# Two attention layers with exact row maxima: one rotation of three PSUM banks for row scores and turned maxima, and the narrow bias products of layer 1 in one run

## The reference, cut to what matters

```python
Q, K, V = split(query @ Wq.T + bq), split(key @ Wk.T + bk), split(value @ Wv.T + bv)   # 16 heads of 16
scores = einsum("bhqd,bhkd->bhqk", Q, K) / 4       # 512 x 1024 for each head and batch
scores = where(mask, -inf, scores)                 # layer 0: a boolean mask
scores = scores + attn_mask                        # layer 1: an additive mask; both: softmax over k
out = einsum("bhqk,bhkd->bhqd", softmax(scores), V) @ Wo.T + bo
x = x + out
```

## Time and profile before

| | |
|---|---|
| median of three runs | 1301.94 us (1301.23 to 1302.68) |
| the profiled execution: own time, span | 1301.66 us, 1299.9 us |
| mean granted TensorE clock | 0.943 |
| TensorE, VectorE, ScalarE, GpSimd busy | 89%, 44%, 35%, 16% of the span |
| steps of layer 0, from the first head product | 104.4 to 343.2 us |
| opening of layer 1 in attend | 672.8 to 707.4 us |
| steps of layer 1 | 707.4 to 967.8 us |

### The profile page before, as it was taken

The page is one execution under the profiler, slowest core; times in us unless marked ns, Lnnn a source line. Parts: engine busy times, 40 slices in busy tenths (PEclk is TensorE's granted clock), DMA queues, the critical chain, the costliest instruction groups (busy, mean ns, idle before and its releaser), DMA issues. The chain is left out here.

```text
span 1299.9 us, 19266 instructions
## 1 busy us (share of the span) xinstructions
PE 1158.5 (89%) x7144; PEld 714.0 (55%) x7144; DVE 568.1 (44%) x1587; ACT 452.6 (35%) x584; POOL 205.3 (16%) x334
## 2 busy tenths in 40 slices
PE   5777999999959999999667999999996499999993
PEld 3432333333447888888533223322225499999993
DVE  5465777774263111112356676666505311111112
ACT  4344666666412111121033455555662011111110
POOL 4362222223100000000013000000200111111110
PEclk9998999999959999999878899999997699999997
DMA  7527222200273334445069022220003699998943
GB/s 222 135 106 174 37 38 37 38 1 1 98 260 49 130 129 138 179 176 137 24 225 173 1 37 38 38 38 1 1 2 131 219 369 313 316 319 317 313 150 106
DMA packets 95878, 169.45 MB, mean 130 GB/s; under 512 B 8529, under 2 KB 65569, under 8 KB 94770
## 3 DMA queue, kind: packets, MB, share of 16 engines
q1 hardware_dynamic: 89570, 157.59, 40.5%
q0 software_dynamic: 2208, 6.03, 1.6%
q10 hardware_dynamic: 4016, 4.72, 1.1%
HBM read 148.34 MB, written 19.79 MB: 129 GB/s over the span
## 5 line engine op out<-in xcount | busy, mean ns | idle before, releaser
L1042 ACT ACTIVATE prob<-st_ps 128x1024 f32<-128x1024 f32 x256 | 261.0, 1025 | 192.9 <-PE st_ps L938 107.7
L131 DVE CUSTOM_DVE_ANT_0 junk<-s_ps,bias_rows,mx 128x512 f32<-128x512 f32 x236 | 172.2, 750 | 72.7 <-PE s_ps L116 72.5
L116 PE MATMUL s_ps<-k_stack,q_stack 97*128 97x512 bf16 x468 | 181.3, 392 | 12.6 <-DMA q_stack<-q_scr 6.6
L930 PE MATMUL st_ps<-q_stack,k_stack 100*128 100x512 bf16 x512 | 185.5, 386 | 6.9 <-ACTq L1021 6.9
L131 DVE CUSTOM_DVE_ANT_0 junk<-s_ps,bias_rows 128x512 f32<-128x512 f32 x232 | 156.2, 690 | 75.9 <-PE s_ps L116 72.7
L1429 PE MATMUL h_ps<-expert_in,w 128*128 (+1 forms) x704 | 155.0, 382 | 2.3 <-PEq L64 2.3
L1429 PEld LDWEIGHTS h_ps<-expert_in,w 128*128 128x128 f32 (+1 forms) x704 | 132.7, 189 | 23.0 <-issue 2.5
L950 PE MATMUL o_ps<-prob,v_unit 128*32 128x512 f32 x1024 | 140.6, 603 | 0.5 <-ACT prob L1042 0.5
L116 PEld LDWEIGHTS s_ps<-k_stack,q_stack 97*128 97x128 bf16 x468 | 45.0, 98 | 166.4 <-DVE mx L131 136.6
L1832 ACT ACTIVATE silu<-gu_ps 128x512 f32<-128x512 f32 x46 | 27.5, 597 | 226.7 <-PE gu_ps L1788 226.7
L935 PE MATMUL st_ps<-bias_hi,ident_bf 128*128 128x512 bf16 x256 | 97.9, 382 | 0.0
(11 more groups left out here) (270 smaller groups left out, 1121.7 us busy)
## 6 DMA issues: line engine op xcount, KB each, us to landing
wg<-in_gateT SPq DMA_DIRECT2D x23, 1024.0 KB
wu<-in_upT SPq DMA_DIRECT2D x23, 1024.0 KB
wd<-in_downT SPq DMA_DIRECT2D x23, 1024.0 KB
w<-in_w SPq DMA_DIRECT2D x16, 1368.0 KB
k_stack<-k_scr SPq DMA_DIRECT2D x96, 128.0 KB, 4.9
w<-in_w SPq DMA_DIRECT2D x8, 1280.0 KB
k_scr<-k_parts SPq DMA_DIRECT2D x24, 256.0 KB, 2.5
q_stack<-q_scr SPq DMA_DIRECT2D x96, 64.0 KB, 4.9
```

The lines of the kernel that those rows point to most:

```text
L116: pe.matmul(self.ps[:, j % 2], stack(self.pr.Q[b], MROW, i % 2, h, slice(qt * P, (qt + 1) * P)), stack(self.pr.K[b], MROW, i % 2, h, slice ...
L131: self.pr.nc.vector.tensor_tensor_reduce(out=self.junk[:, j % 2], in0=self.ps[:, j % 2], in1=self.m.bias_rows[:, qt, half * 512:(half + 1) ...
L930: pe.matmul(st_ps[:, h], stack(K[b], ROWS, i % 2, h, slice(kt * P, (kt + 1) * P)), stack(Q[b], ROWS, i % 2, h, slice(0, SQ)), start=True, ...
L1042: nc.scalar.activation(prob[:, kt % 2, 2 * hp:2 * hp + 2], st_ps[:, 2 * hp:2 * hp + 2], ACT.Exp).then_inc(exp_done, 1)
```

## The change

`RowPass` (of `attend`; the opening of layer 0 keeps it, with `FirstMax` for its turns) and `MaxSteps` become one class, `RowRing`. It writes out the order of all row products and turns of a layer as TensorE will issue them, and gives them three banks in rotation. Each waits until the one three places before is read: a job's maximum, or a turn's write. The bank `m_ps` is gone; a turn no longer waits for the write of the turn before as such. GpSimd's five steps are the same (`split_max`). Two semaphore increments of a job (`passed`) and a memset fall away. In layer 1, the order of a step becomes h0 r0 h1 h2 r1 h3 r2 b0 b1 b2 b3, turn, weigh, r3. Layer 0 keeps its order.

```diff
+TURN_AT = (3, 6)
-            pe.wait_ge(self.done, u * 32 + j + 1)
-            pe.matmul(self.ps[:, j % 2], stack(self.pr.Q[b], MROW, i % 2, h, slice(qt * P, (qt + 1) * P)),
+class RowRing:
+    BANKS = 3
...
+        order = []
+        if first == 0:
+            order += [("job", 0, j) for j in range(32)] + [("turn", 0, 0), ("turn", 0, 1)]
+        for u in range(NU):
+            for kt in range(KT):
+                order += [("job", *x) for x in plan[u, kt][:3]]
+                if u + 1 < NU and kt in TURN_AT:
+                    order.append(("turn", u + 1, TURN_AT.index(kt)))
+                order += [("job", *x) for x in plan[u, kt][3:]]
+        self.order, self.place = order, {x: n for n, x in enumerate(order)}
+    def bank(self, *x):
+        return self.place[x] % self.BANKS
+    def free(self, pe, *x):
+        n = self.place[x] - self.BANKS
+        if n >= 0:
+            kind, u, i = self.order[n]
+            if kind == "job":
+                pe.wait_ge(self.done, u * 32 + i + 1)
+            else:
+                pe.wait_ge(self.row_done, (u - self.first) * 2 + i + 1)
...
     def turn(self, pe, u, c2):
-        k = (u - self.first) * 2 + c2
-        pe.wait_ge(self.cut_done, k + 1)
-        if k >= 1:
-            pe.wait_ge(self.row_done, k)
+        pe.wait_ge(self.cut_done, (u - self.first) * 2 + c2 + 1)
+        self.free(pe, "turn", u, c2)
...
                     else:
                         head_scores(u, kt, 0)
+                        row.scores(pe, jobs[:1])
                         head_scores(u, kt, 1)
-                        row.scores(pe, jobs[:1])
-                        head_bias(kt, 0)
-                        head_bias(kt, 1)
                         head_scores(u, kt, 2)
                         row.scores(pe, jobs[1:2])
                         head_scores(u, kt, 3)
                         row.scores(pe, jobs[2:3])
-                        head_bias(kt, 2)
-                        head_bias(kt, 3)
-                    if u + 1 < NU and kt in (3, 6):
-                        top.turn(pe, u + 1, kt // 6)
+                        for h in range(HG):
+                            head_bias(kt, h)
+                    if u + 1 < NU and kt in TURN_AT:
+                        row.turn(pe, u + 1, TURN_AT.index(kt))
                     if kt or u:
                         weigh(*divmod(u * KT + kt - 1, KT))
                     row.scores(pe, jobs[3:])
```

More of the change, by code:

```diff
@@ L155, in stack, with __init__, scores, maxima @@
     return X[0:rows, bass.ds(k, 1), h, cols].rearrange("r o c -> r (o c)")
[L158 to L165, removed]
+class RowRing:
+    BANKS = 3
+    def __init__(self, pr, c, l, m, first, plan):
+        self.pr, self.l, self.m, self.first = pr, l, m, first
+        self.junk = pr.sb(c, f"junk{l}", [P, self.BANKS, 512], F32)
+        self.ps = pr.banks(c, f"s_ps{l}", self.BANKS)
+        self.ready, self.done = pr.sem(f"s_ready{l}"), pr.sem(f"mx_done{l}")
+        self.init, self.chain, self.cut_done = (pr.sem(f"{x}{l}") for x in ("mpart_init", "chain", "mp_done"))
+        self.turned, self.row_done = pr.sem(f"mt_done{l}"), pr.sem(f"mrow_done{l}")
+        order = []
[18 more added lines that the diff above has]
+                pe.wait_ge(self.row_done, (u - self.first) * 2 + i + 1)
+    def scores(self, pe, jobs):
+        for u, j in jobs:
+            i, b = divmod(u, B)
+            h, half, qt = j // 8, j % 8 // 4, j % 4
+            self.free(pe, "job", u, j)
+            pe.matmul(self.ps[:, self.bank("job", u, j)],
+                      stack(self.pr.Q[b], MROW, i % 2, h, slice(qt * P, (qt + 1) * P)),
+                      stack(self.pr.K[b], MROW, i % 2, h, slice(half * 512, (half + 1) * 512)),
+                      start=True, stop=True).then_inc(self.ready, 1)
+    def maxima(self, dve, jobs):
+        mx = self.m.mx
+        for u, j in jobs:
+            b = u % B
+            h, half, qt = j // 8, j % 8 // 4, j % 4
+            dve.wait_ge(self.ready, u * 32 + j + 1)
+            first = -4 * BIG
+            if half:
+                dve.wait_ge(self.done, u * 32 + j + 1 - 4)
+                first = mx[:, b, h, qt, 0:1]
+            self.pr.nc.vector.tensor_tensor_reduce(out=self.junk[:, self.bank("job", u, j)],
+                                                   in0=self.ps[:, self.bank("job", u, j)],
+                                                   in1=self.m.bias_rows[:, qt, half * 512:(half + 1) * 512],
+                                                   scale=1.0, scalar=first, op0=ALU.add, op1=ALU.max,
+                                                   accum_out=mx[:, b, h, qt, half:half + 1]).then_inc(self.done, 1)
@@ L893, in _ @@
                 if l == 1:
-                    top.fill(pool)
+                    row.fill(pool)
                     pool.wait_ge(m.ctx_in, 48)
@@ L928, in head_scores @@
                         if kt == 0:
-                            top.written(pe, u, h // 2)
+                            row.written(pe, u, h // 2)
                     pe.matmul(st_ps[:, h], stack(K[b], ROWS, i % 2, h, slice(kt * P, (kt + 1) * P)),
@@ L971, in _ @@
                         value(n)
-                    top.turn(pe, 0, 0)
-                    top.turn(pe, 0, 1)
+                    row.turn(pe, 0, 0)
+                    row.turn(pe, 0, 1)
                     pe.wait_ge(load[1], 16 * N_DMA)
@@ L1027, in _ @@
                         nc.scalar.activation(m.vals[:, n], st_ps[:, n % 4, 0:D], ACT.Copy).then_inc(v_read, 1)
-                    top.write(act, 0, 0)
-                    top.write(act, 0, 1)
+                    row.write(act, 0, 0)
+                    row.write(act, 0, 1)
                 def evacuate(u):
@@ L1045, in _ @@
                             evacuate(u - 1)
-                        if u + 1 < NU and kt in (3, 6):
-                            top.write(act, u + 1, kt // 6)
+                        if u + 1 < NU and kt in TURN_AT:
+                            row.write(act, u + 1, TURN_AT.index(kt))
                 evacuate(NU - 1)
```

87 lines of the change are left out of this document (55 added, 32 removed).

## The result

The changed kernel takes 1284.97 us (median of 4 runs, 1283.46 to 1285.45), the kernel before in the same session 1302.31 (4 runs, 1301.23 to 1303.16): ratio 0.9865, 95% interval 0.9848 to 0.9882. The profiled execution took 1284.8 us, span 1283.1.

What follows compares the result with a forecast made beforehand. TensorE's own sequence was taken to bound layer 1's steps; -3.0 - 2.5 + 0.6 - 2.4 - 9.0 + 3.9 + 1.3 = -11.1 us from 1301.66 gave 1290.6, median 1290.8 us, range 1285 to 1297.5.

Steps and rivals of the forecast that it cites:

- Steps of layer 1: Units 1 to 6, 45 steps with row products: one narrow-shape entry and exit go, 3.90 to 3.70 us, -9.0 us.
- the switches stay: Rival, 8%: the 0.20 us a step belongs to something else, steps stay 3.90 and only banks pay; 1299 us.
- ScalarE behind h2: Layer 1 steps: pair 1's exponential frees h2 at 4.51 to 4.59 us, due at 4.58, so it just fits.
- ScalarE sets every step: Rival, 18%: with the upper start and answer times (0.72, 0.14) ScalarE paces layer 1's steps, 5.2 us more; 1296 us.
- The exponential waits for the end of the whole run: Rival, 4%: pair 0 starts 0.44 us later, layer 1 steps take 4.07 against 3.90; 1310 us.
- Turns: Units 1 to 6: r1' waits for ScalarE's late write, 0.35 us at each of 11 turns, +3.9 us.
- The write costs nothing: Rival, 12%: the turn's write goes earlier or r1' comes later, saving 3.9 us and 1 in unit 0; 1286 us.
- Steps without row products: Layer 1's 11 last such steps: ScalarE's circle sets 3.19 us instead of 3.03, +1.3 us (up to +2.8).
- Unit 0: First unit of layer 1: bank gains 1.4 us, order 1.7, table load costs some 0.7; together -2.4 us (0 to -4).
- Layer 0: Order kept; 27 of 53 steps lose a 0.11 us wait before the third row product, -3.0 us (0 to -3.7).
- The opening: Start of layer 1: eight maxima take 5.5 us instead of 6.21, second turn gains 0.1; -2.5 us (-1 to -3.3).
- The clock: Half-clock stretch in layer 1: steps begin 2.5 us earlier, costing +1.25 us if it stays, 0 if it moves; +0.6 taken.

Runs made afterwards that it cites:

- experiment 6: Changed kernel, but VectorE instead of ScalarE writes layer 1's turned maxima, the two opening turns included; 1282.13 us, ratio 0.9855 to the kernel before.
- experiment 5: Changed kernel with the old order (two runs of eight bias products) only in layer 1's 11 steps without row products; 1283.86 us, ratio 0.9859.
- 9: Kernel before plus 18 and 3 unread filler products on TensorE ahead of layer 1's two opening turns; 1295.88 us, ratio 0.9956.
- 10: Changed kernel with three banks but layer 1's old step order, plus 18 and 3 filler products ahead of the opening turns; 1282.01 us, ratio 0.9849.
- 7: Changed kernel plus 18 and 3 unread filler products on TensorE ahead of layer 1's two opening turns; 1282.37 us, ratio 0.9850.
- experiment 8: Changed kernel with old order in steps without row products, VectorE writing layer 1's turns, and filler products before the opening turns; 1274.15 us, ratio 0.9787.
- experiment 1: Changed kernel with three banks kept but the old order of a step in layer 1; 1291.03 us, ratio 0.9909 to the kernel before.
- experiment 2: Kernel before, with its two banks for row products, given only layer 1's new step order; 1319.31 us, ratio 1.0117.

## Why the prediction missed, by its steps

**Steps of layer 1: right.** 3.70 and 4.14 were forecast and measured; an entry and an exit of the narrow shape go, 0.20. By the Trainium skill (TensorEngine Tiling (Array Packing), Key Properties) changing the tiling mode drains TensorE. The trace agrees in that each change has a cost: 0.09 in (0.31 for 0.22, 792.22 to 792.53) and, in the rows of before, 0.10 to 0.11 out; no row shows a drain itself. Sixteen narrow products cost 0.87 in one run (792.53 to 793.40). The rival *the switches stay* is out. The forecast counted 45 steps from one length; three of them were longer before, for a bank, and gave 0.8 more: -5.9 for -5.1.

**ScalarE behind h2: fits, barely.** Of the two unknowns the start came out at its upper value (0.73) and the answer at its lower (0.05): h2 is free at 1.85 + 0.73 + 0.92 + 1.02 + 0.05 = 4.57, due at 4.58. *ScalarE sets every step* needed both upper values, 0.14 for the answer; no step of units 1 to 6 shows that. *The exponential waits for the end of the whole run* is out: it starts 0.73 behind the run's start, with 0.14 of the run to go.

**Turns: right.** 0.37 at r1' for 0.35; experiment 6 takes the wait away and the 0.37 goes. *The write costs nothing* is out. The write starts 1.04 behind the second exponential (796.95 + 0.92 = 797.87, to 798.91), so the overlap that the prediction cited from the Trainium skill (ScalarE: Activation LUTs, What ACT_TABLE_LOAD costs) shows between two exponentials (1.94 for two of 1.02) and not before this copy.

**Steps without row products: mechanism right, size off.** ScalarE's circle sets them as reckoned, 3.26 for 3.19, since pair 0 starts at 0.73 and not 0.66: +2.4 for +1.3, inside the bound given (+2.8). Shown by experiment 5.

**Unit 0: the sum near by luck, both its parts wrong.** At the full clock, -1.4 for the bank was -4.3 (9 against 10), and -1.0 for order and table load together was +2.4 (10 against 7); net -1.9 for -2.4. The waits for VectorE vanished wholly with the third bank; of 4.9 the forecast had left 1.6 of them standing and put waits for writes beside them. It had laid the waits out for both edits at once, and then called them the bank's, which is why it saw no loss in the order. ScalarE holds the first step up by 1.5 at the full clock (5.32 against 3.84): 0.3 is the wait for the opening's second write (5.00 without it, experiment 8), and 1.2 the table load, for which 0.7 stood. Under the half clock the first step is only 0.2 longer with the order (6.62 against 6.41).

**Layer 0: a little more than reckoned**, -3.8 for -3.0: beside the 27 steps that lose 0.11, the others fall from 3.74 to 3.72 and the turns from 4.15 to 4.12, the case kept in its bound (-3.7).

**The opening: mis-sized.** The step that failed says "VectorE needs 8 x 0.69 = 5.5". 0.69 is busy time; maxima in a row overlap and start 0.61 and 0.68 apart. Eight take 5.20, TensorE's own pace, which the forecast had worked out (5.24) and kept only as a bound: (6.21 - 5.20) x 3.4 = -3.4 where -2.4 stood. From the first row product to the last value product the trace has -3.7 (26.2 to 22.5). The turns gave 0.6 for 0.1 (2.76 and 3.16 from first turn to first head product in the two executions of before, 2.39 in both of after). Together -4.3 for -2.5, a miss of 1.8.

**The clock: the step that failed most.** "If the stretch stays where it is, 2.5 us more of it fall on steps at half pace, +1.25; if it moves along, 0. I take +0.6." It moved along, 705.1 to 697.6, and the term was not 0. Experiments 7 and 9 price it: 6.1 before, 3.6 after, so -2.5 for +0.6, a miss of 3.1 and the largest. Two things were wrong in the step. It took what a half-clock stretch costs from the stretch alone, apart from the table load in the same first step; but the two cover each other, and that is 1.4 of the 2.5 (1.30 for 2.70 in the first step). And it took the length as given, though it named another length as a sign of being wrong: the stretch came out at 13.7 us for 17.1, 12.0 for 14.8 in steps, which goes with the other 1.1. The length was not even given in the kernel before (17.1 and 20.5 in two executions). The bank alone does not shorten it (17.1 in experiment 1), nor the order alone (17.1 in experiment 2), and both together do, in all four profiled executions that have them and no filler (the changed kernel twice, experiments 5 and 6). Why 13.7 is not settled: the change starts it elsewhere and packs the first steps otherwise, and no run here separates the two.

**What it comes to.** 3.1 (clock) + 1.8 (opening) + 0.8 (layer 0) + 0.8 (units 1 to 6), less 1.1 (last steps) and 0.5 (unit 0), is 4.9: from -11.1 to -15.9 but for rounding. At the full clock the order of layer 1 is worth next to nothing: -9.2 in the steps, +4.1 at turns, +2.4 without row products, +2.4 in unit 0, and the loops of experiments 10 and 7 differ by 0.2. With the half clock, as the kernels ran, it brought 3.4 (257.4 to 254.0), because the stretch costs 3.2 less with it (3.6 for 6.8). What paid is the third bank, some 4 us in each of layer 0, the opening and unit 0, and this lower cost of the half clock.

## What to carry to other kernels

Where an engine's operations overlap, take its pace from the distance between starts; a third buffer is worth the whole distance down to the next engine's pace, which must be worked out too. Price a half-clock stretch by filling the idle time before it in both kernels: its length can change with the edit, and it costs less in a step that another engine holds up anyway, so the two losses can't simply be added. And where a new order gains in one kind of step, cost it in each other kind (turns, last steps, first unit) and keep the old one there: used everywhere the order brought 0.2 us; used only where it pays, with the write on another engine and the filler, it stands in a version 13 us faster than the change.

## What the runs showed of the chip

- TensorE's granted clock fell to 0.50 (1.2 GHz) after 4.35 us in which TensorE waited, and a turn (0.61 us of products from 694.2 to 697.6), and stayed there for 13.7 us although TensorE was busy in 12.63 of 13.60 us; in the same work of the kernel before it stayed for 17.1 and 20.5. With 4.15 of 4.50 us busy in its place it didn't fall.
- The same copy of 4 x 1024 bf16 out of PSUM takes VectorE 0.70 us and ScalarE 1.02.
- Two executions of one kernel differ by 2 us in the start of layer 0's steps (102.45 and 104.42), though the steps themselves repeat to 0.2 (236.5 and 236.4 from first head product to last `weigh`).
